# A graph network's head re-ordered: pair list read first, attention column sums moved back, x and bias added by TensorE

## What is computed

```python
edge_index = jnp.stack([src, dst])
x = _layernorm(x + _L0_gnn_ref(x, edge_index, W_l, W_r, b_r))          # mean of neighbours @ W_l.T + x @ W_r.T + b_r
x = _layernorm(x + _L1_gnn_ref(x, edge_index, W, att_src, att_dst, bias, ln_gamma, ln_beta))   # GAT, 4 heads
x = _layernorm(x + _L2_gnn_ref(x, W1, b1, W2, b2, edge_index, 16))     # edge MLP: relu([x_i, x_j - x_i] @ W1 + b1) @ W2 + b2
x = _layernorm(x + _L3_gnn_ref(x, edge_index, weight, attn_l, attn_r)) # heads weighted by a softmax over heads
```

## Time and profile before

| | us |
|---|---|
| median of 3 runs (496.94 to 498.1) | 497.29 |
| the profiled execution, its own time | 498.36 |
| its span | 496.6 |
| TensorE busy | 387.1 (78%) |
| VectorE busy | 307.4 (62%) |
| GpSimd busy | 275.7 (56%) |
| ScalarE busy | 203.4 (41%) |
| mean granted TensorE clock | 0.914 |

### The profile page before, as it was taken

The page is one execution under the profiler, slowest core; times in us unless marked ns, Lnnn a source line. Parts: engine busy times, 40 slices in busy tenths (PEclk is TensorE's granted clock), DMA queues, the critical chain, the costliest instruction groups (busy, mean ns, idle before and its releaser), DMA issues.

```text
span 496.6 us, 5501 instructions
## 1 busy us (share of the span) xinstructions
PE 387.1 (78%) x1407; PEld 203.8 (41%) x1408; DVE 307.4 (62%) x595; ACT 203.4 (41%) x494; POOL 275.7 (56%) x277
## 2 busy tenths in 40 slices
PE   5635755699657776796999997799999999989820
PEld 3212212387613432343555553355444344437620
DVE  4289999777699978625454442445444954445426
ACT  3435976404766541165334443134334343103310
POOL 5365765005595540027677777777777777746040
PEclk9959899999958787797999999799999999999985
DMA  6531221000000000046577776777777767730001
GB/s 166 197 88 41 68 59 47 1 1 0 3 0 0 0 1 0 21 146 196 158 207 213 210 211 210 209 213 204 214 207 210 199 199 211 211 105 1 1 5 54
DMA packets 23638, 55.69 MB, mean 112 GB/s; under 512 B 5505, under 2 KB 10820, under 8 KB 23606
## 3 DMA queue, kind: packets, MB, share of 16 engines
q0 software_dynamic: 15344, 47.56, 33.9%
q1 hardware_dynamic: 6934, 6.51, 4.4%
q10 hardware_dynamic: 1328, 1.23, 1.0%
HBM read 52.87 MB, written 2.40 MB: 111 GB/s over the span
## 4 chain that ended last, share of the span: by engine, by line
PE 34%; DVE 26%; POOL 19%; issue 8%; DMA 5%; ACT 4%; SPq 2%; DVEq 0%; ACTq 0%; POOLq 0%
PE ps L1211 32%; POOL arena L480 16%; DVE arena L865 9%; DVE q_sb L1040 3%; DVE arena L860 2%; DVE x L1021 2%; DMA g<-in_L_gnn_weight 2%; DMA arena<-q_table,t_odd 2%; DVE stats L933 1%; POOL al_g L510 1%; POOL adj L480 1%; ACT xT L529 1%; PE ps L1225 1%; ACT arena L529 1%; DMA al_table<-al_sb 1%
## 5 line engine op out<-in xcount | busy, mean ns | idle before, releaser
L1120 DVE TENSOR_TENSOR arena<-arena,ps 128x1024 f32<-128x1024 f32 x83 | 101.3, 1221 | 107.8 <-DMA arena<-q_table,t_odd 84.7
L1211 PE MATMUL ps<-arena,hot 128*128 128x512 f32 x332 | 163.6, 616 | 1.1 <-DVE arena L1120 1.1
L480 POOL DMA_INDIRECT arena<-q_table,t_even x83 | 79.2, 954 | 68.1 <-DMA q_table<-q_sb 40.0
L480 POOL DMA_INDIRECT arena<-q_table,t_odd x83 | 80.3, 968 | 25.3 <-issue 25.3
L1211 PE MATMUL ps<-parts,hotT 125*128 x166 | 75.9, 540 | 9.6 <-DVE arena L1120 8.6
L1211 PEld LDWEIGHTS ps<-arena,hot 128*128 128x128 f32 x332 | 58.1, 195 | 51.3 <-issue 44.2
L689 ACT ACTIVATE hot<-h_sb,ones 128x128 fp32r<-128x128 f32 x83 | 33.3, 401 | 107.3 <-PE ps L1211 107.3
L1211 PEld LDWEIGHTS ps<-parts,hotT 125*128 125x128 f32 x166 | 30.5, 198 | 59.5 <-issue 59.1
L1211 PE MATMUL ps<-arena 128*128 128x376 f16 (+1 forms) x178 | 33.0, 327 | 22.1 <-DVE arena L865 14.9
L865 DVE TENSOR_SCALAR arena<-iota,t_column,t_weight 128x376 f16<-128x376 f16 x140 | 45.6, 397 | 0.0
L442 POOL DMA_INDIRECT arena<-hot_table,t_even x28 | 30.6, 1092 | 14.9 <-issue 9.4
(11 more groups left out here) (232 smaller groups left out, 524.2 us busy)
## 6 DMA issues: line engine op xcount, KB each, us to landing
arena<-q_table,t_even POOLq DMA_INDIRECT x83, 3.7
arena<-q_table,t_odd POOLq DMA_INDIRECT x83, 3.7
q_table<-q_sb SPq DMA_DIRECT2D x5, 224.0 KB
w_sb<-in_L_gnn_W SPq DMA_DIRECT2D x1, 1024.0 KB, 10.4
x<-in_x ACTq DMA_DIRECT2D x1, 560.0 KB
out<-x SPq DMA_DIRECT2D x5, 112.0 KB
w_sb<-in_L_gnn_W SPq DMA_DIRECT2D x1, 512.0 KB, 10.9
arena<-hot_table,t_even POOLq DMA_INDIRECT x28, 2.7
```

Of the source, the lines that this page charges most:

```text
L480: pool.indirect_dma_start(to, None, q_dram[:, :], bass.IndirectOffsetOnAxis(ap=index, axis=0)).then_inc(done, 16)
L1120: V.tensor_tensor(both, both, ps[:, 5 + i % 2, :].unsqueeze(1).to_broadcast([128, 2, HID]), ALU.max).then_inc(maxed, 1)
L1211: return nc.tensor.matmul(o, a, b, start=start, stop=stop, skip_group_check=True)
```

## The change

The four products and sums of the attention columns are split. The two for g1 are still multiplied in the head by GpSimd, and summed by VectorE behind its last group of the count stage. The two for g3 are multiplied and summed behind the second norm, in adj in place of q_sb, after w1_dif, which moves there too. `linear` gets x and b_r added by TensorE: two products with the unit matrix and one of ones (1 row) with b_r; GpSimd's two additions and the semaphore xr_ready go. b_r is loaded as one row by ScalarE's queue, where SP broadcast it to 128 partitions. Linear block 3 moves behind group 1. TensorE waits for folded at 2 in layer 1 and at 4 in layer 3; GpSimd's gathers into adj wait for folded at 4.

```diff
@@ prod
-        prod = [q_sb[:, n, :].rearrange("p (c f) -> p c f", c=DC) for n in range(4)]
+        prod = [q_sb[:, n, :].rearrange("p (c f) -> p c f", c=DC) for n in range(2)]
+        prod += [adj[:, n, 0:HID].rearrange("p (c f) -> p c f", c=DC) for n in range(2)]
@@ sync
-            for n, ap in enumerate((b_r, bias1, gamma, beta, b2)):
+            for n, ap in enumerate((bias1, gamma, beta, b2), 1):
@@ gpsimd, head
-            for n in range(4):
-                if n == 2:
-                    pool.wait_ge(g3_loaded, 16)
+            def weigh_columns(n):
                 g = g1 if n < 2 else g3
                 nc.gpsimd.tensor_tensor(prod[n], g[:, :, 0:D], att[:, n, :].unsqueeze(1).to_broadcast([128, DC, D]),
                                         ALU.mult).then_inc(atts_ready, 1)
-            pool.wait_ge(w1_loaded, 16)
-            nc.gpsimd.tensor_tensor(w1_dif[:, :, :], w1_sb[:, 0:2, :], w1_sb[:, 2:4, :], ALU.subtract).then_inc(dif_ready, 1)
-
-            pool.wait_ge(x_loaded, 32)
-            pool.wait_ge(rows_loaded, 96)
-            nc.gpsimd.tensor_tensor(tmp[0:NP, :, :], x0[0:NP, :, :], rows[0:NP, 0, :].unsqueeze(1).to_broadcast([NP, NT, D]),
-                                    ALU.add).then_inc(pool_step, 1)
+
+            for n in range(2):
+                weigh_columns(n)
@@ gpsimd, between the gathers of groups 3 and 4
-                pool.wait_ge(pool_step, 2)
-                pool.wait_ge(lin_read, 2 * NT)
-                nc.gpsimd.tensor_tensor(xr[0:NP, :, :], xr[0:NP, :, :], tmp[0:NP, :, :], ALU.add).then_inc(xr_ready, 1)
@@ gpsimd, ahead of the bias for layer 1
+                pool.wait_ge(rows_loaded, 80)
@@ gpsimd, behind the GAT scores
+                pool.wait_ge(x_ready, 2 * NT)
+                pool.wait_ge(w1_loaded, 16)
+                nc.gpsimd.tensor_tensor(w1_dif[:, :, :], w1_sb[:, 0:2, :], w1_sb[:, 2:4, :], ALU.subtract).then_inc(dif_ready, 1)
+                pool.wait_ge(g3_loaded, 16)
+                for n in range(2, 4):
+                    weigh_columns(n)
@@ gpsimd, at FIRSTS_AT (pair 30)
                             pool.wait_ge(first_rows, 1)
+                            pool.wait_ge(folded, 4)
@@ scalar
+            act.dma_start(br_row[:, :], b_r.rearrange("(c f) -> c f", c=1)).then_inc(br_loaded, 16)
...
-                        if g < 3:
-                            linear_out(NT - 3 + g)
+                        if 2 <= g < 4:
+                            linear_out(NT - 4 + g)
@@ vector, head; the sums are now a function
-            for n_att in range(4):
+            def fold(n_att):
@@ vector, behind the last group of hots
+                    for n_att in range(2):
+                        fold(n_att)
@@ vector, first norm
-                dve.wait_ge(xr_ready, 1)
+                dve.wait_ge(lin_read, 2 * NT)
@@ vector, behind x2_b2 (L1102), ahead of the first p_sb (L1107)
+                for n_att in range(2, 4):
+                    fold(n_att)
@@ tensor, linear
                 for c in range(DC):
-                    last = mm(ps[0:NP, lin_bank(b), :], xT[:, c, b * NP:(b + 1) * NP], w_lrT[:, c, :], c == 0, c == DC - 1)
-                last.then_inc(lin_done, 1)
+                    mm(ps[0:NP, lin_bank(b), :], xT[:, c, b * NP:(b + 1) * NP], w_lrT[:, c, :], c == 0, False)
+                for c in range(DC):
+                    mm(ps[0:NP, lin_bank(b), D + c * 128:D + (c + 1) * 128], xT[:, c, b * NP:(b + 1) * NP], ident[:, :], False, False)
+                mm(ps[0:NP, lin_bank(b), D:2 * D], ones[0:1, 0:NP], br_row[0:1, :], False, True).then_inc(lin_done, 1)
@@ tensor
+            pe.wait_ge(br_loaded, 16)
             linear(0)
...
             pe.wait_ge(list_read, 3)
-            linear(3)
...
+                        if g == 1:
+                            linear(NT - 2)
                         if g == 2:
                             last_linear()
...
-                pe.wait_ge(folded, 4)
+                pe.wait_ge(folded, 2)
...
+                pe.wait_ge(folded, 4)
-                pe.wait_ge(pool_step, 3 + NT)
+                pe.wait_ge(pool_step, 2 + NT)
```

More of the change, by code:

```diff
@@ L100, in program @@
         b1_row = sb("b1_row", [128, HID], f32)
+        br_row = sb("br_row", [1, D], f32)
         src_i = sb("src_i", [128, ET], i32)
@@ L252, in program @@
         att_loaded, w1_loaded, w2_loaded = sem("att_loaded"), sem("w1_loaded"), sem("w2_loaded")
-        rows_loaded, e_loaded = sem("rows_loaded"), sem("e_loaded")
+        rows_loaded, e_loaded, br_loaded = sem("rows_loaded"), sem("e_loaded"), sem("br_loaded")
         filled, consts, pool_step = sem("filled"), sem("consts"), sem("pool_step")
@@ L260, in program @@
         atts_ready, folded = sem("atts_ready"), sem("folded")
-        dif_ready, xr_ready = sem("dif_ready"), sem("xr_ready")
+        dif_ready = sem("dif_ready")
         wT_done, wT_copied = sem("wT_done"), sem("wT_copied")
@@ L502, in pool_layers @@
                 nc.gpsimd.tensor_copy(dst_row_f, dst_row_i).then_inc(pool_step, 1)
-                pool.wait_ge(pool_step, 3)
+                pool.wait_ge(pool_step, 2)
                 pool.wait_ge(edges_done, 1)
```

## The result

The changed kernel takes **489.02 us** (median of 4 runs, 488.55 to 489.96), the kernel before, beside it, 497.13 us (4 runs, 496.94 to 498.1). The ratio is 0.9833, with a 95% interval of 0.981 to 0.9856. The forecast was 489.0, and the difference of the two medians is 8.1 us. The profiled execution took 489.96 us, its span is 488.1 us; before these were 498.36 and 496.6.

A forecast was written before the change was run, and what follows sets the result against it. No engine bounds the whole span; VectorE bounds the count stage at 3.84 us a group. 498.36 - 8.3 gives 490.0 us profiled, less 1.07 for the median: 489.0 us; 8 in 10 between 485.5 and 492.5.

The forecast's parts named there:

- The sum's size: Whole change: VectorE ends the count stage at 81.6 instead of 89.93 us, and the execution shortens by the same 8.3 us.
- The column sums leave the head: Head, VectorE: list read at 17.2 instead of 26.42 us, building from 20.7; upper bound of the gain 15.5 us.
- What is late next: Head: the store of hot_table behind SP's weight loads becomes the gate; first gather at 28.8 instead of 34.21 us.
- So group 1 starts at 33.25: Count stage, TensorE: group 1 starts 4.45 us after the first gather at 28.8 us.
- Group 1 runs at the 1.2 GHz level: Count stage, TensorE: idle some ten microseconds before, group 1 runs at half clock and takes 3.75 us.
- rival B: Count stage: inserted linear blocks run at half clock, 2.8 us longer each; 491.8 us with one, 494.6 with both; chance 0.15.
- The three waits: Count stage, VectorE: waits 4.7 us for group 1's buffer, then 1.1 and 1.2 us behind the inserted linear blocks.
- GpSimd's two additions ... that they blocked VectorE is in the sum: Removed additions of x and b_r (2.90, 2.94 us) were off the chain but blocked VectorE; 2.9 us of 8.3 at L865.
- w1_dif and the g3 columns: hidden by 10 and 11 us: Behind the second norm: moved GpSimd work is done at 208.3 us, before TensorE's products (216.04) and the gathers (219.40).
- A: Head: the store is not the gate, VectorE waits little; 13 us saved, 484 us; chance 0.07.
- C: Count stage: TensorE's clock stays at 1.2 GHz throughout, about 4.0 us a group; 8 us slower, 505 us; chance 0.03.
- D: Later stages: one absorbs the gain; outright no gain chance 0.03, with plus or minus 1.5 us allowed for the clock.

The follow-up runs named there:

- the early store: Changed kernel with SP's store of hot_table issued ahead of the loads of g3, W1, W2 and the edge sources; ratio 0.9766 of the kernel before.
- block 0 behind the list: Changed kernel with linear block 0 moved from ahead of the pair list to behind it and nothing else; 487.63 us, ratio 0.9836 of the kernel before.
- TensorE kept at work: Changed kernel with 36 products of zeros on TensorE between the clearing of the counts and group 1; 486.75 us, ratio 0.9821 of the kernel before.
- the kernel they were compared with: Changed kernel with VectorE's two sums for g1 back in the head, ahead of the list's read; ratio 0.9851 of the kernel before.
- w1_dif three times: Changed kernel with GpSimd computing w1_dif three times behind the second norm; 488.07 us, ratio 0.9813 of the kernel before.

## Why the prediction held, step by step

**The sum's size.** Forecast for the count stage 8.3 us, measured 7.05; for the whole profiled execution 8.3, measured 8.40. The agreement is better than the working, and to that extent luck: about 1.2 us were lost more than I had written down, and 1.2 us came back in the edge layer, where I had written nothing but a margin. The same kernel's marks differ by 1.3 us between two executions, so neither is more than scatter and small errors of the terms. Timed again, the changed kernel was 7.1 us below the kernel before (490.06 against 497.20) and not 8.1.

**"The column sums leave the head"**: list read at 17.2, measured 18.11 and 17.67. Two causes. The added products cost 1.15 us a block (0.53 and 0.62 from the starts 19.82, 20.35, 20.97) and not 0.95. The product with one row of weights took 0.62 us, where half of a 512-column product, with 128 rows, takes 0.46: the single row made it no cheaper. And in the first profile one of the index loads was some 1 us later. The read took 2.5 us (predicted 2.6), t_even 0.19.

**"What is late next"**: right in kind and shown, since the early store alone moved the first gather by 4.8 us and block 0 behind the list moved it not at all. In size: 28.8 forecast, 29.45 and 29.06 measured. The DMA engines fell silent by 28.1 us, earlier than I took, but the gather came some 1.4 us behind that, not 0.5. So the term that I had put at 0.5 us was mis-sized, and an earlier end of the bytes hid a part of it. The same 1.4 us stand in the second run of this kernel (last bytes by 27.7, gather at 29.06), and 1.3 in the kernel with block 0 moved alone (27.7, 29.03).

**"So group 1 starts at 33.25"**: 34.26; the first gather took 1.53 instead of 1.19, and the stretch behind it 4.81 instead of 4.45.

**"Group 1 runs at the 1.2 GHz level"**: 3.75 forecast, 3.94 and 3.39 measured, 2.14 with TensorE kept at work: right. The 3.48 us group that I had cited for it had waited for ScalarE, not for a DMA; group 1 here did wait for a DMA, 9.35 us long. Of the inserted blocks I had taken block 3 at full clock; it ran at 2.37 instead of 1.88 for its large products, then full clock: of rival B's 2.8 us for a block, 0.5 came true. In the second profile none of it did (1.88), in the kernel with block 0 moved alone 1.1 us (2.96).

**The three waits** of 4.7, 1.1 and 1.2 us: measured 5.05, 1.29, 0.85 and, again, 4.72, 0.86, 0.85. From group 7 on VectorE waited no more. One L868 run took 3.34 us, where none over 3.2 was forecast. The blocks behind groups 1 and 2 cost what the second and third wait say, 2.05 us in the kernel they were compared with. Putting them ahead took 3.6 us off the mark, since group 1 then also started at full clock.

**"GpSimd's two additions ... that they blocked VectorE is in the sum"**: shown by putting them back, and undersized. I had counted 2.9 us for L452's effect, and said that its own time was not on the chain. That is right for the kernel before, where VectorE was late enough to hide the gathers behind it. With VectorE early, the old addition would have held the gathers of group 4, 2.4 us of waits more. So removing it is what lets the early list pay. Whether block 3 behind group 1 adds to that was not tried by itself. The Trainium skill (SBUF — State Buffer, "Who interferes with whom") was cited for the exclusive port. These runs agree: the L865 and L874 runs that lie beside a GpSimd tensor operation take 0.9 to 5.4 us more than 3.1, those beside none at most 0.3 more.

**"w1_dif and the g3 columns: hidden by 10 and 11 us"**: right in that nothing reached the gathers. 4.7 us more of it are hidden too.

**Rivals.** A fell (the store is the gate), C fell (clock 1.00 from 60 to 80 us), D did not occur. What stays open is why the early-store kernel had 123.6 us from VectorE's adj to the first q_table gather, where the others have 124.8 to 128.5, and why the kernel with w1_dif three times was faster than the changed one.

## What to carry to other kernels

When you free an engine early, find what its lateness had hidden: here VectorE started 11.8 us earlier and kept 7.05, and the rest lay in a store at the end of a queue of loads and in blocks put between dependent groups; moved to where their engines idled, they gave 8 us more. If GpSimd works beside VectorE, count each of its tensor operations at VectorE's price too, and look again at what stands behind each of its waits once VectorE is earlier: here the rest of the change was worth 1.4 us with GpSimd's additions in place, and the whole change, without them, 7 to 8 us.

## What the runs showed of the hardware that I had not expected

- **The first gather varies:** it took 1.53 and 1.50 us in the changed kernel, 1.73 with TensorE kept at work, 2.05 with the first sums in the head, 1.19 before and with the early store, where later ones take 0.95. The cause was not tried.
- **Small operations of VectorE (5 elements in each of 125 partitions) wait for the end of a GpSimd operation beside them:** L1097, L1099 and L1101 took 1.41, 1.19 and 1.19 us beside w1_dif and the products, where they took 0.16 to 0.17 before; 2.32 us for one of the same size with w1_dif three times. There another of them (L1102), at the moment when one w1_dif ended and the next began, took 0.17.
- **The last byte of a store is not its end:** 1.3 to 1.7 us passed from the silence of the DMA engines to the gather that waited for it, in six executions (1.4 in both of the changed kernel).
- **The clock fell at different points:** in two executions of the changed kernel TensorE's last work ahead of group 1 ended within half a microsecond of the same place, and the granted clock was still 1.00 at 28.2 us in one and 0.50 by 27.2 in the other. Group 1 started at half clock in both. With the blocks ahead it started at 1.00 behind a wait of 3.39 us, and the clock fell to 0.50 while it ran.
- **A DMA's issue is slow behind large ones:** the same store took 0.87 us to issue ahead of the loads of g3, W1 and W2, in all four kernels with it there, and 7.50 to 8.89 us behind them.
